# Split-operand products for Q, K, V and Wo, column-tiled gates and an earlier bias fold in a transformer and MoE kernel

## The chip, the cores and the metric

One core of a Trainium2 chip (trn2). The time is the device time of one execution in microseconds: 970.05 for the kernel before, the median of 3 runs (969.35 to 970.36).

## The reference

Video is 8 x 512 x 256 in f32. Two layers follow one another: linear attention with random features (16 heads of 16, 64 features a head) with a feed-forward part behind it, and a mixture of 8 experts. Around the parts stand layer norms and residuals. Cut to what matters:

```python
q = split(video @ Wq.T + bq); k = split(video @ Wk.T + bk); v = split(video @ Wv.T + bv)
qp = softmax_kernel(q, proj, is_query=True)      # 16 heads, 64 features each
kp = softmax_kernel(k, proj, is_query=False)
k_sum = jnp.sum(kp, axis=2)
denom = jnp.einsum('bhnm,bhm->bhn', qp, k_sum)
ctx = jnp.einsum('bhnm,bhnd->bhmd', kp, v)
out = jnp.einsum('bhnm,bhmd->bhnd', qp, ctx) / denom[..., None]
attn = out.transpose(0, 2, 1, 3).reshape(b, n, d) @ Wo.T + bo
x = layer_norm(video + attn, g2, be2)
ff = jax.nn.relu(x @ W1.T + b1) @ W2.T + b2
y = layer_norm(x + ff, g3, be3)
...
scores = jax.nn.softmax(xf @ gate_w.T, axis=-1)  # 8 experts
vals, idx = jax.lax.top_k(scores.T, k)           # 512 rows for each expert
# each expert: layer norm of its rows, fc1, gelu, fc2, times score, added at idx
```

## The kernel before

Tokens go in 8 batches of 512 (4 tiles of 128 tokens; 256 features are 2 tiles of 128). All five engines run programs of their own, ordered by semaphores. Each program is a loop over `body(i, f, u)`, a pipeline three batches deep: `i` is the batch in attention, `f` the batch in the feed-forward part (i - 1), `u` the batch in the last norm and the gates (i - 2). Bodies 0 and 1 and the last two lack some of the parts. The order inside a body is written out by hand on each engine, so an instruction that waits holds everything behind it on its engine. Behind the batches come the selection of 512 rows for each expert, the eight experts, and the last norm.

PSUM is cut into pA (2 banks, attention), pX (4 banks, random features, also written as pXall) and pF (2 banks, feed-forward and gates). pA and pF are handed on in turn: PE waits in `slot_a` and `slot_f` until the engine that takes the previous content has done so.

The order on PE around the change, in body i: K and Q (`by_features`, 512 columns, f32), V (`by_tokens`, 256 columns, f32), the turn of x2 of batch i - 1, the random features of k (`features`), two turns of heads, and between the further features the hidden layer of batch i - 1 in eight pieces (`hidden`, L1413, with `by_halves`), then its second product (`ff_out`), the maxima (`turn_kmax`, `spread_kmax`, `turn_tops`), the turned features, the context, the key sum (L1560), `attention_out` (L1434), the turns of xf and of oT, the gates (L1473), the turn of at, `turn_x(i + 1)`, and Wo (L1601). In body 0 the fold of be2 into the bias of the hidden layer stands at the end (L1602 to L1608: 32 instructions with one column each).

`by_halves` (L1378) takes operands that are split into an upper part, rounded to f32r, and a lower part, the rest. It sums three products: low x high, high x low, high x high. The hidden layer and the experts work like this; K, Q, V and Wo are plain f32 products.

VectorE (DVE) subtracts the lower halves (x2T_lo, L957), takes the maxima (L888, L917), subtracts the key bias (k_sub, L912), adds up statistics (L857, L861), writes xn (L882), x2, z and xf (L867), divides the heads (`heads_out`, L1010 and L1013), and adds r (L1049). `sums_of_context` (csum, csum_own, obias; L923 to L927) stands just ahead of xn in body 0. ScalarE (ACT) copies from PSUM (L474, L479, L484) and takes the exponentials. GpSimd (POOL) takes the roots (`root`, L719 and L721), sums kp over tokens (L770) and applies the scale and shift of the norms. In body 0, after `root(0, 1)`, it waits for the second fold_ready and then scales W1 by g2 and splits it:

```python
for c in range(C):
    nc.gpsimd.tensor_scalar(w1_raw[:, c], w1_raw[:, c], g2_c[:, c:c + 1], None, ALU.mult).then_inc(w1_split, 1)
pool.wait_ge(w1_split, C)
nc.gpsimd.tensor_copy(w1_hi[:], w1_raw).then_inc(w1_split, 1)
pool.wait_ge(w1_split, C + 1)
nc.gpsimd.tensor_tensor(w1_lo[:], w1_raw, w1_hi[:].bitcast(F32), ALU.subtract).then_inc(w1_split, 1)
```

Body 1 then adds be2 to b2 on POOL, takes `root(1, 0)` of the sum r of batch 0, and DVE makes x2 with it. `hidden(0)` of batch 0 waits for the split W1.

## Time and the profile before

| | |
|---|---|
| time, median of 3 | 970.05 us |
| profiled execution | 970.41 us, span 968.6 us |
| mean granted TensorE clock | 0.900 |
| PE busy | 762.2 us (79%), 5561 instructions |
| PE weight loads | 581.5 us (60%) |
| DVE busy | 595.6 us (61%) |
| ACT busy | 410.6 us (42%) |
| POOL busy | 352.9 us (36%) |
| chain that ended last | PE 62%, DVE 13%, DMA 6%, ACT 6%, POOL 6%, issue 5% |

Busy times are averages over stages. The attention and feed-forward stage reaches to about 630 us, the selection to about 700, the experts to about 925. The chain is followed back from the last instruction, at each step to what released it or to the instruction before it on its engine.

### The profile page before, as it was taken

Reading aid. Unit: us, or ns where it says so; the run is one execution under the profiler, and the core shown is the slowest. Engines: PE = TensorE matmul, PEld = TensorE weight load, DVE = VectorE, ACT = ScalarE, POOL = GpSimd, SP = SyncE. Lnnn points to the kernel's source line nnn. Section 1 sums busy time; section 2 is a strip of 40 time slices with the busy share of each in tenths; the row PEclk is TensorE's granted clock in tenths of the full one; section 3 lists DMA queues with packets and bytes.
Section 4 is the critical chain, followed back from the end, with each engine's and each line's share of the span. In section 5 each row is a group of like instructions: output and inputs, shape, how many; then the busy total and the mean of one; then the engine's idle time right before and its main releaser. Section 6 shows DMA issues by size and latency. Waiting matters only on the chain.

```text
span 968.6 us, 15201 instructions
## 1 busy us (share of the span) xinstructions
PE 762.2 (79%) x5561; PEld 581.5 (60%) x5561; DVE 595.6 (61%) x1426; ACT 410.6 (42%) x594; POOL 352.9 (36%) x299
## 2 busy tenths in 40 slices
PE   5578999999999999999999967211459989999900
PEld 2345856767767758668577656211348888888800
DVE  2722735857857957848758562588836656666445
ACT  2632634735636536637447321100045434455324
POOL 3136333514416405425335151100134444544346
PEclk9798999999999999999999979555569999999955
DMA  7000010011011020110100102220053555555274
GB/s 208 1 23 1 1 45 1 2 66 46 23 44 44 22 84 3 48 61 0 65 23 1 66 23 83 71 94 0 7 169 92 153 132 170 138 132 135 31 213 150
DMA packets 61530, 64.63 MB, mean 67 GB/s; under 512 B 9264, under 2 KB 58160, under 8 KB 61488
## 3 DMA queue, kind: packets, MB, share of 16 engines
q1 hardware_dynamic: 54384, 55.37, 17.4%
q0 software_dynamic: 6144, 8.52, 5.0%
q8 instruction: 27, 0.44, 0.2%
q10 hardware_dynamic: 960, 0.17, 0.1%
q14 instruction: 15, 0.12, 0.0%
HBM read 42.95 MB, written 21.10 MB: 66 GB/s over the span
## 4 chain that ended last, share of the span: by engine, by line
PE 62%; DVE 13%; DMA 6%; ACT 6%; POOL 6%; issue 5%; POOLq 0%; DVEq 0%; SPq 0%; ACTq 0%
PE pF L1382 10%; PE pX L1660 10%; PE pF L1424 9%; PE pA L1368 6%; PE pA L1375 5%; PE pX L1464 5%; DMA xg<-row_scratch,idx_g 4%; PE pX L1393 4%; PE pA L1353 3%; DVE qe L1108 3%; PE pX L1382 3%; POOL xg L799 2%; PE pA L1434 2%; PE pF L1477 2%; PE pF L1353 2%
## 5 line engine op out<-in xcount | busy, mean ns | idle before, releaser
L1424 PE MATMUL pF<-w,h 128*128 128x256 f32 x512 | 116.0, 380 | 0.0
L1424 PEld LDWEIGHTS pF<-w,h 128*128 128x128 f32 x512 | 95.6, 190 | 13.8 <-issue 1.4
L719 POOL TENSOR_SCALAR ve<-mv 128x4 f32<-128x4 f32 x40 | 9.1, 228 | 247.0 <-DVE mv L861 246.4
L807 POOL DMA_INDIRECT acc_scratch<-at,idx_s x32 | 51.6, 1613 | 107.3 <-DVE at L1216 100.6
L799 POOL DMA_INDIRECT xg<-row_scratch,idx_g x32 | 47.3, 1478 | 99.0 <-issue 86.0
L630 ACT ACTIVATE h<-pX,b1cur 128x512 f32<-128x512 f32 x64 | 44.1, 690 | 88.9 <-DVE b1cur L1227 75.4
L1660 PE MATMUL pX<-w_lo,h_hi 128*128 128x256 f32 x256 | 73.7, 288 | 0.8 <-issue 0.8
L1660 PE MATMUL pX<-w_hi,h_lo 128*128 128x256 f32 x256 | 73.0, 285 | 0.0
L1660 PE MATMUL pX<-w_hi,h_hi 128*128 128x256 f32 x256 | 72.9, 285 | 0.0
L867 DVE TENSOR_SCALAR z<-z,mv,rstd 128x256 f32<-128x256 f32 x64 | 62.3, 1034 | 7.0 <-POOL rstd L721 7.0
L479 ACT ACTIVATE h<-pF,b1c 128x512 f32<-128x512 f32 x64 | 44.2, 691 | 48.4 <-PE pF L1382 48.4
L1199 DVE TENSOR_TENSOR h_lo<-h,h_hi 128x512 fp32r<-128x512 f32 x64 | 42.9, 690 | 30.5 <-ACT h_hi L622 30.5
L1382 PE MATMUL pF<-x2T_hi,w_lo 128*128 128x512 f32 x128 | 55.1, 430 | 1.4 <-DVE x2T_lo L957 1.4
L1382 PE MATMUL pX<-x2T_hi,w_lo 128*128 128x512 f32 x128 | 51.8, 405 | 2.8 <-DVE x2T_lo L1248 2.8
L1382 PE MATMUL pX<-x2T_lo,w_hi 128*128 128x512 f32 x128 | 51.6, 403 | 0.0
L1382 PE MATMUL pF<-x2T_hi,w_hi 128*128 128x512 f32 x128 | 51.5, 403 | 0.0
L1382 PE MATMUL pX<-x2T_hi,w_hi 128*128 128x512 f32 x128 | 51.4, 401 | 0.0
L1382 PE MATMUL pF<-x2T_lo,w_hi 128*128 128x512 f32 x128 | 51.2, 400 | 0.0
L1660 PEld LDWEIGHTS pX<-w_lo,h_hi 128*128 128x128 f32 x256 | 49.7, 194 | 1.4 <-issue 1.4
L888 DVE TENSOR_REDUCE mxk<-kp 128x16 f32<-128x1024 f32 x32 | 37.3, 1209 | 21.4 <-ACT kp L489 21.4
L1660 PEld LDWEIGHTS pX<-w_hi,h_lo 128*128 128x128 f32 x256 | 49.7, 194 | 0.0
L1660 PEld LDWEIGHTS pX<-w_hi,h_hi 128*128 128x128 f32 x256 | 49.6, 194 | 0.0
(260 smaller groups left out, 1860.0 us busy)
## 6 DMA issues: line engine op xcount, KB each, us to landing
kp<-fc1T SPq DMA_DIRECT2D x8, 1024.0 KB, 7.9
w<-fc2T SPq DMA_DIRECT2D x8, 1024.0 KB, 8.0
xin<-video SPq DMA_DIRECT2D x8, 512.0 KB, 3.9
x<-video SPq DMA_DIRECT2D x8, 512.0 KB, 4.5
x_scratch<-x SPq DMA_DIRECT2D x8, 512.0 KB, 2.9
acc_scratch<-xf SPq DMA_DIRECT2D x8, 512.0 KB, 3.0
row_scratch<-y SPq DMA_DIRECT2D x8, 512.0 KB, 3.0
qp<-x_scratch SPq DMA_DIRECT2D x2, 1024.0 KB, 10.5
```

The lines of the kernel that those rows point to most:

```text
L479: nc.scalar.activation(dst, pF[n % 2][:], func, **kw).then_inc(done, 1)
L630: nc.scalar.activation(h[:, n, :], pM[n % M_SLOTS], ACT.Gelu_apprx_tanh, bias=b1cur[:, n:n + 1]).then_inc(he_ready, 1)
L799: pool.indirect_dma_start(xg[:, g, :], None, row_d, bass.IndirectOffsetOnAxis(ap=idx_g[:, g:g + 1], axis=0)).then_inc(gathered, 16)
L807: pool.indirect_dma_start(acc_d, bass.IndirectOffsetOnAxis(ap=idx_s[:, g:g + 1], axis=0), og[:, g, :], None, compute_op=ALU.add).then_inc( ...
L867: ins = nc.vector.tensor_scalar(dst[:, t, :], src[:, t, :], mv[k][:, t, 0:1], rstd[k][:, t:t + 1], ALU.subtract, ALU.mult)
L1353: return nc.tensor.transpose(dst, src, ident[:])
L1368: ins = nc.tensor.matmul(dst[:, t2 * D:(t2 + 1) * D], xt[:, k, tok(2 * m + t2)], w[:, k, :], start=(k == 0), stop=(k == ks - 1))
L1375: ins = nc.tensor.matmul(dst[:], w[:, k, tok(n)], xt[:, k, :], start=(k == 0), stop=(k == ks - 1))
L1382: ins = nc.tensor.matmul(dst[:], w_[:, k, tok(n)], x_[:, k, :], start=(m == 0), stop=(m == len(parts) - 1))
L1424: ins = nc.tensor.matmul(slots[m][:, half * D:(half + 1) * D], h[:, k, tok(2 * m + half)], w2[:, k, :], start=(k == 0), stop=(k == FC - 1))
L1464: ins = nc.tensor.matmul(pXall[:, a, :], w_[rows], x_[rows], start=(n == 0), stop=(n == 2), tile_position=(32 * a, 0))
L1660: ins = nc.tensor.matmul(pM[2 + m][:, t2 * D:(t2 + 1) * D], h_[:, k, tok(2 * m + t2)], w_[:, k, :], start=(k == 0 and j == 0), stop=(k == ...
```

## The change

Q, K, V and Wo are computed as three f32r products of split operands. The weights are split once at the start: ACT copies the upper halves after all four raw weights have come (now into qp's memory), DVE subtracts. x and the heads (aT) are split in each batch: ACT's copy gives the upper half, two DVE subtractions each the lower one. Wo's result and the turned x go to the four-bank buffer pX instead of pA. The gates take 32 columns of weights, four token tiles side by side in four column tiles, with the experts along the partitions; DVE copies the result and PE turns it back (`turn_gates`). The fold of be2 moves from the end of body 0 on PE to a place behind `spread_kmax` of the same body, and DVE's addition of it with it, behind bo_b. v and the turned xf get places in qe, aT_hi and aT_lo take the place of xT and v, xT_hi and xT_lo share memory with x2T_hi and x2T_lo, and in the expert stage xg lies in kp and xga in oT. The diff, without the renamed semaphores and tensors:

```diff
-        wq, wk, wv, wo = (sb(n, [P, C, D]) for n in ("wq", "wk", "wv", "wo"))
+        wq_hi, wk_hi, wv_hi, wo_hi = (sb(n, [P, C, D], F32R) for n in ("wq_hi", "wk_hi", "wv_hi", "wo_hi"))
+        wq_lo, wk_lo, wv_lo, wo_lo = (sb(n, [P, C, D], F32R) for n in ("wq_lo", "wk_lo", "wv_lo", "wo_lo"))
-        gate = sb("gate", [P, C, P])
+        gate = sb("gate", [P, C, 32])
...
+        wq, wk, wv, wo = (qp[:].rearrange("p a b -> p (a b)")[:, k * C * D:(k + 1) * C * D].rearrange("p (c n) -> p c n", c=C)
+                          for k in range(4))
+        xfT = qe[:].rearrange("p a b -> p (a b)")[:, 4 * N:6 * N].rearrange("p (c n) -> p c n", c=C)
+        v = qe[:].rearrange("p a b -> p (a b)")[:, 6 * N:8 * N].rearrange("p (t d) -> p t d", t=TT)
...
+        xT_hi, xT_lo = x2T_hi, x2T_lo
+        gT = sb("gT", [P, P])
...
-        xgT_hi, xgT_lo, xga = x2T_hi, x2T_lo, aT
+        xgT_hi, xgT_lo, xga = x2T_hi, x2T_lo, oT[:, 0:C]
-        xg = sb("xg", [P, GT, ROW])
+        xg = kp_f[:, 0:GT * ROW].rearrange("p (g r) -> p g r", g=GT)
...
-                sp.dma_start(w[:], src.rearrange("(c p) n -> p c n", p=P)).then_inc(done, 16)
+            for w, src in ((wk, WkT), (wq, WqT), (wv, WvT), (wo, WoT)):
+                sp.dma_start(w, src.rearrange("(c p) n -> p c n", p=P)).then_inc(wqkvo_in, 16)
...
-                    nc.scalar.activation(xT[:, c, :], pA[c][:], ACT.Copy).then_inc(xT_ready, 1)
+                    nc.scalar.activation(xT_hi[:, c, :], pXall[:, c, :], ACT.Copy).then_inc(xT_ready, 1)
...
+                    if isinstance(i, int) and i == 0:
+                        act.wait_ge(wlo_ready, 4)
                     exp_q(i, 0)
                     exp_q(i, 1)
...
+            act.wait_ge(wqkvo_in, 16 * 4)
+            for hi, w in ((wk_hi, wk), (wq_hi, wq), (wv_hi, wv), (wo_hi, wo)):
+                nc.scalar.activation(hi[:], w, ACT.Copy).then_inc(whi_ready, 1)
             act.wait_ge(const_ready, N_CONST)
             xT_copy(0)
             act.wait_ge(bqk_in, 16 * 2)
...
+            def rest_of_weight(n, w, lo, hi):
+
+                dve.wait_ge(whi_ready, n + 1)
+                nc.vector.tensor_tensor(lo[:], w, hi[:].bitcast(F32), ALU.subtract).then_inc(wlo_ready, 1)
+
+            def rest_of_x(i):
+                for c in range(C):
+                    dve.wait_ge(xT_ready, i * C + c + 1)
+                    nc.vector.tensor_tensor(xT_lo[:, c, :], pXall[:, c, :], xT_hi[:, c, :].bitcast(F32), ALU.subtract).then_inc(xl_ready, 1)
+
+            def rest_of_heads(i):
+
+                for c in range(C):
+                    dve.wait_ge(aT_ready, i * C + c + 1)
+                    nc.vector.tensor_tensor(aT_lo[:, c, :], pA[(J_AT + c) % 2][:], aT_hi[:, c, :].bitcast(F32), ALU.subtract).then_inc(al_ready, 1)
...
                     if isinstance(i, int) and i == 0:
                         dve.wait_ge(fold_ready, 1)
                         nc.vector.tensor_tensor(bo_b[:], bo_b[:], pF[1][:, 0:D], ALU.add).then_inc(bias_ready, 1)
+                        dve.wait_ge(wff_in, 16 * N_WFF)
+                        dve.wait_ge(fold_ready, 2)
+                        nc.vector.tensor_tensor(b1c[:], b1c[:], pF[0][:, 0:FC], ALU.add).then_inc(bias_ready, 1)
...
-                    for m in range(2):
-                        dve.wait_ge(u_ready, u * U_JOBS + J_G + m + 1)
-                        nc.vector.tensor_copy(lg[:, 2 * m:2 * m + 2, :],
-                                              pF[m][:, 0:2 * P].rearrange("p (a b) -> p a b", a=2)[:, :, 0:E]).then_inc(lg_ready, 1)
-                    dve.wait_ge(lg_ready, 2 * (u + 1))
-                    su.link(nc.vector.tensor_reduce(lmx[:], lg[:], AX_X, ALU.max))
-                    nc.vector.tensor_tensor(lg[:], lg[:], lmx[:].unsqueeze(2).to_broadcast([P, TT, E]), ALU.subtract).then_inc(ls_ready, 1)
+                    dve.wait_ge(u_ready, u * U_JOBS + J_G + 1)
+                    nc.vector.tensor_copy(gT[:], pF[0][:, 0:P]).then_inc(lg_ready, 1)
+                if i is not None:
+                    rest_of_heads(i)
+                if more:
+                    rest_of_x(i + 1)
+                if u is not None:
+                    dve.wait_ge(u_ready, u * U_JOBS + J_G + 2)
+                    logits = pF[1][:, 0:P].rearrange("p (t x) -> p t x", t=TT)[:, :, 0:E]
+                    su.link(nc.vector.tensor_reduce(lmx[:], logits, AX_X, ALU.max))
+                    nc.vector.tensor_tensor(lg[:], logits, lmx[:].unsqueeze(2).to_broadcast([P, TT, E]), ALU.subtract).then_inc(lg_ready, 1)
                 if i is not None:
                     dve.wait_ge(xnb_ready, i + 1)
                     for m in range(2):
                         dve.wait_ge(a_ready, i * A_JOBS + J_WO + m + 1)
-                        nc.vector.tensor_tensor(r[:, 2 * m:2 * m + 2, :], pA[m][:].rearrange("p (a b) -> p a b", a=2),
+                        nc.vector.tensor_tensor(r[:, 2 * m:2 * m + 2, :], pXall[:, 2 + m, :].rearrange("p (a b) -> p a b", a=2),
                                                 xnb[:, 2 * m:2 * m + 2, :], ALU.add).then_inc(r_ready, 1)
                     sa.end()
...
-                if isinstance(i, int) and i == 0:
-                    dve.wait_ge(wff_in, 16 * N_WFF)
-                    dve.wait_ge(fold_ready, 2)
-                    nc.vector.tensor_tensor(b1c[:], b1c[:], pF[0][:, 0:FC], ALU.add).then_inc(bias_ready, 1)
 
             ln1_stats(0)
             ln1_norm(0)
+            rest_of_weight(0, wk, wk_lo, wk_hi)
             dve.wait_ge(wproj_in, 16 * HG)
             nc.vector.tensor_scalar(projbd[:], projbd[:], NORM, None, ALU.mult).then_inc(proj_ready, 1)
+            rest_of_x(0)
+            rest_of_weight(1, wq, wq_lo, wq_hi)
+            rest_of_weight(2, wv, wv_lo, wv_hi)
+            rest_of_weight(3, wo, wo_lo, wo_hi)
             dve.wait_ge(bvo_in, 16 * 2)
...
-                       + [(aT_ready, 2, c) for c in range(2)] + [(r_ready, 2, m) for m in range(2)])
+                       + [(al_ready, 2, c) for c in range(2)] + [(r_ready, 2, m) for m in range(2)])
...
             def slot_a(i, n):
 
-                if J_WO <= n and not (isinstance(i, int) and i == B - 1):
-                    pe.wait_ge(xT_ready, (i + 1) * C + n - J_WO + 1)
-                elif n < 2:
-                    s, per, k = a_taker[A_JOBS + n - 2]
+                if J_WO <= n:
+
+                    return pXall[:, 2 + n - J_WO, :]
+                if n < 2:
+                    s, per, k = a_taker[J_AT + n]
                     wait(pe, s, (i - 1) * per + k + 1)
                 else:
                     s, per, k = a_taker[n - 2]
@@ -1319,10 +1354,9 @@
             def turn_x(i):
 
                 pe.wait_ge(xn_ready, (i + 1) * TT)
+                wait(pe, qp_ready, i * G)
                 for c in range(C):
-
-                    wait(pe, aT_ready, (i - 1) * C + c + 1)
-                    turn_tokens(pA[c], xn, c).then_inc(t_ready, 1)
+                    turn_tokens(pXall[:, c, :], xn, c).then_inc(t_ready, 1)
...
             def slot_x(i, n):
 
                 if n == J_XK:
-                    wait(pe, qp_ready, i * G)
+                    pe.wait_ge(xl_ready, (i + 1) * C)
+                    wait(pe, r_ready, i * 2)
...
-            def by_tokens(dst, xt, w, m, ks):
-
+            def by_tokens(dst, x_hi, x_lo, w_hi, w_lo, m):
+
+                parts = [(k, x_, w_) for x_, w_ in ((x_hi, w_lo), (x_hi, w_hi), (x_lo, w_hi)) for k in range(C)]
                 for t2 in range(2):
-                    for k in range(ks):
-                        ins = nc.tensor.matmul(dst[:, t2 * D:(t2 + 1) * D], xt[:, k, tok(2 * m + t2)], w[:, k, :],
-                                               start=(k == 0), stop=(k == ks - 1))
-                return ins
-
-            def by_features(dst, w, xt, n, ks):
-
-                for k in range(ks):
-                    ins = nc.tensor.matmul(dst[:], w[:, k, tok(n)], xt[:, k, :], start=(k == 0), stop=(k == ks - 1))
+                    for j, (k, x_, w_) in enumerate(parts):
+                        ins = nc.tensor.matmul(dst[:, t2 * D:(t2 + 1) * D], x_[:, k, tok(2 * m + t2)], w_[:, k, :],
+                                               start=(j == 0), stop=(j == len(parts) - 1))
                 return ins
...
-                def gates(m):
-                    s = slot_f(f, u, "u", J_G + m)
-                    for t2 in range(2):
-                        for c in range(C):
-                            ins = nc.tensor.matmul(s[:, tok(t2)], xfT[:, c, tok(2 * m + t2)], gate[:, c, :],
-                                                   start=(c == 0), stop=(c == C - 1))
+                def gates():
+
+                    s = slot_f(f, u, "u", J_G)
+                    for c in range(C):
+                        for t in range(TT):
+                            ins = nc.tensor.matmul(s[32 * t:32 * t + 32, 0:P], gate[:, c, :], xfT[:, c, tok(t)],
+                                                   start=(c == 0), stop=(c == C - 1), tile_position=(0, 32 * t))
                     ins.then_inc(u_ready, 1)
 
+                def turn_gates():
+
+                    s = slot_f(f, u, "u", J_G + 1)
+                    pe.wait_ge(lg_ready, 2 * u + 1)
+                    turn(s[:, 0:P], gT[:]).then_inc(u_ready, 1)
+
                 at_first(f, pe)
                 if att:
                     pe.wait_ge(xT_ready, (i + 1) * C)
-                    for j0, w, w_in in ((J_K, wk, wk_in), (J_Q, wq, wq_in)):
-                        first_batch(w_in)
+                    pe.wait_ge(xl_ready, (i + 1) * C)
+                    for n, (j0, hi, lo) in enumerate(((J_K, wk_hi, wk_lo), (J_Q, wq_hi, wq_lo))):
+                        first_batch(wlo_ready, n + 1)
                         for c in range(G):
-                            by_features(slot_a(i, j0 + c), w, xT, c, C).then_inc(a_ready, 1)
-                    first_batch(wv_in)
+                            by_halves(slot_a(i, j0 + c), hi, lo, xT_hi, xT_lo, c).then_inc(a_ready, 1)
+                    first_batch(wlo_ready, 3)
                     for m in range(2):
-                        by_tokens(slot_a(i, J_V + m), xT, wv, m, C).then_inc(a_ready, 1)
+                        by_tokens(slot_a(i, J_V + m), xT_hi, xT_lo, wv_hi, wv_lo, m).then_inc(a_ready, 1)
...
+                    if isinstance(i, int) and i == 0:
+                        pe.wait_ge(w1_in, 16)
+                        pe.wait_ge(wff_in, 16 * N_WFF)
+                        for n in range(FC):
+                            for c in range(C):
+                                ins = nc.tensor.matmul(pF[0][:, n:n + 1], w1_raw[:, c, tok(n)], be2_c[:, c:c + 1], start=(c == 0), stop=(c == C - 1))
+                        ins.then_inc(fold_ready, 1)
...
                 if gt_:
                     pe.wait_ge(xfT_ready, (u + 1) * C)
-                    gates(0)
-                    gates(1)
+                    gates()
                 if att:
                     pe.wait_ge(at_ready, (i + 1) * TT)
                     for c in range(C):
                         turn_tokens(slot_a(i, J_AT + c), at, c).then_inc(a_ready, 1)
                     if not (isinstance(i, int) and i == B - 1):
                         turn_x(i + 1)
+                if gt_:
+                    turn_gates()
+                if att:
                     pe.wait_ge(aT_ready, (i + 1) * C)
-                    first_batch(wo_in)
+                    first_batch(wlo_ready, 4)
                     for m in range(2):
-                        by_tokens(slot_a(i, J_WO + m), aT, wo, m, C).then_inc(a_ready, 1)
-                if isinstance(i, int) and i == 0:
-                    pe.wait_ge(w1_in, 16)
-                    pe.wait_ge(wff_in, 16 * N_WFF)
-                    for n in range(FC):
-                        for c in range(C):
-                            ins = nc.tensor.matmul(pF[0][:, n:n + 1], w1_raw[:, c, tok(n)], be2_c[:, c:c + 1], start=(c == 0), stop=(c == C - 1))
-                    ins.then_inc(fold_ready, 1)
+                        if m == 0:
+                            pe.wait_ge(al_ready, (i + 1) * C)
+                        by_tokens(slot_a(i, J_WO + m), aT_hi, aT_lo, wo_hi, wo_lo, m).then_inc(a_ready, 1)
```

## Rows read from the trace of the kernel before

**Rows 1.** Chain that ended last, middle batches: start us, us, what (x instructions)

```profile
216.65 3.69 PE pA L1368 x16
...
264.14 0.57 PE pA L1560 x16
...
280.26 1.79 PE pF L1477 x16
282.05 0.45 PE pA L1353 x4
...
284.58 3.72 PE pA L1368 x16
288.30 6.87 PE pA L1375 x16
295.17 3.45 PE pA L1368 x16
```

**Rows 2.** The same chain in the expert stage

```profile
729.84 11.71 PE pX L1660 x96
```

**Rows 3.** Timeline of DVE, middle batch: start us, us, then idle before it

```profile
293.86 1.35 DVE L867 TENSOR_SCALAR x<-r,mv,rstd 128x256 f32<-128x256 f32 x4
...
299.77 1.29 DVE L957 TENSOR_TENSOR x2T_lo<-pF,x2T_hi 128x512 fp32r<-128x512 f32 x2 [2.88 <-ACT x2T_hi L479]
...
322.47 7.68 DVE L867 TENSOR_SCALAR z<-z,mv,rstd 128x256 f32<-128x256 f32 x4
...
348.55 0.42 DVE L1013 TENSOR_TENSOR at<-pA,rden 128x256 f32<-128x256 f32 x1
```

**Rows 4.** Timeline of ACT, middle batch

```profile
350.48 1.08 ACT L474 ACTIVATE aT<-pA 128x512 f32<-128x512 f32 x2 [3.95 <-PE pA L1353]
```

**Rows 5.** Timeline of POOL, middle batch

```profile
322.02 2.76 POOL L770 TENSOR_TENSOR sq<-kp 128x1024 f32<-128x1024 f32 x1 [8.63 <-ACT kp L515]
324.86 4.82 POOL L770 TENSOR_TENSOR sq<-sq,kp 128x1024 f32<-128x1024 f32 x2
```

**Rows 6.** Chain that ended last, batches 0 and 1

```profile
11.40 1.28 ACT L484
...
13.83 8.66 PE pA L1375 x16
...
43.33 1.13 PE pX L1353 x4
...
74.11 3.48 PE pF L1607 x32
77.76 5.69 POOL h L781 x2
...
85.49 4.52 POOL w_lo L785
...
93.74 1.97 PE pF L1353 x8
...
99.32 2.80 PE pF L1382 x12
```

**Rows 7.** Timeline of DVE in batch 0

```profile
60.49 1.46 DVE L882 TENSOR_SCALAR xn<-xin,mv,rstd 128x256 f32<-128x256 f32 x4
64.82 0.26 DVE L1010 RECIPROCAL rden<-pA 128x16 f32<-128x16 f32 x1 [2.88 <-PE pA L1353]
```

**Rows 8.** Timeline of POOL in batch 0

```profile
55.92 1.05 POOL L721 TENSOR_TENSOR rstd<-ve,mhalf 128x4 f32<-128x4 f32 x1
```

**Rows 9.** Windows: stretch, length, then each engine's busy us, granted clock, DMA

```profile
38.00:45.00 7.00, 1.39 (x10) 0.88 (x5) 6.58 (x7) 4.82 (x6) 0.00 (x0) 0.50 0.00 0
```

**Rows 10.** Chain that ended last, behind the last batch

```profile
623.99 3.79 PE pF L1477 x16
```

**Rows 11.** Instructions and transfers of tile wo

```profile
L401 SPq DMA_DIRECT2D wo<-WoT x1: 473/473/473, 2.9 to 2.9; - x1
...
DMA to landing us min/median/max: 5.5/5.5/5.5
```

More of the change, by code:

```diff
@@ L252, in build, with early @@
         with ExitStack() as first_stages:
-            def early(name, shape):
-                return first_stages.enter_context(nc.sbuf_tensor(name, shape, F32))
+            def early(name, shape, dt=F32):
+                return first_stages.enter_context(nc.sbuf_tensor(name, shape, dt))
             xin = early("xin", [P, TT, D])
@@ L258, in build @@
             xnb = early("xnb", [P, TT, D])
-            xT = early("xT", [P, C, N])
+            aT_hi = early("aT_hi", [P, C, N], F32R)
+            aT_lo = early("aT_lo", [P, C, N], F32R)
             kT = early("kT", [P, G, N])
             qT = early("qT", [P, G, N])
-            v = early("v", [P, TT, D])
             r = early("r", [P, TT, D])
@@ L278, in build @@
         vel, rsl, nmr = (sq_f[:, 384 + 64 * n:384 + 64 * n + B * TT].rearrange("p (k t) -> p k t", k=B) for n in range(3))
-        wk_in, wq_in, wv_in, wo_in = (sem(f"w{n}_in") for n in "kqvo")
+        wqkvo_in, whi_ready, wlo_ready = sem("wqkvo_in"), sem("whi_ready"), sem("wlo_ready")
+        xl_ready, al_ready = sem("xl_ready"), sem("al_ready")
         bqk_in, bvo_in = sem("bqk_in"), sem("bvo_in")
@@ L310, in build @@
         xfT_ready, lg_ready = sem("xfT_ready"), sem("lg_ready")
-        ls_ready, le_ready, sc_ready = sem("ls_ready"), sem("le_ready"), sem("sc_ready")
+        le_ready, sc_ready = sem("le_ready"), sem("sc_ready")
         x1_out, xf_out, y_out, sc_out = sem("x1_out"), sem("xf_out"), sem("y_out"), sem("sc_out")
@@ L399, in _ @@
             load_x(0)
-            for w, src, done in ((wk, WkT, wk_in), (wq, WqT, wq_in), (wv, WvT, wv_in), (wo, WoT, wo_in)):
-                sp.dma_start(w[:], src.rearrange("(c p) n -> p c n", p=P)).then_inc(done, 16)
+            for w, src in ((wk, WkT), (wq, WqT), (wv, WvT), (wo, WoT)):
+                sp.dma_start(w, src.rearrange("(c p) n -> p c n", p=P)).then_inc(wqkvo_in, 16)
             sp.dma_start(w1_raw, W1T.rearrange("(c p) n -> p c n", p=P)).then_inc(w1_in, 16)
@@ L597, in body @@
                     for c in range(C):
-                        take_a(i, J_AT + c, aT[:, c, :], ACT.Copy, aT_ready)
+                        take_a(i, J_AT + c, aT_hi[:, c, :], ACT.Copy, aT_ready)
                     if not (isinstance(i, int) and i == B - 1):
@@ L1406, in body, with first_batch @@
                 att, ff, gt_ = i is not None, f is not None, u is not None
-                def first_batch(w_in):
+                def first_batch(ready, value):
                     if isinstance(i, int) and i == 0:
-                        pe.wait_ge(w_in, 16)
+                        pe.wait_ge(ready, value)
                 def hidden(n):
@@ L1511, in body @@
                     if isinstance(i, int) and i == 0:
-                        pe.wait_ge(wo_in, 16)
+                        pe.wait_ge(wqkvo_in, 16 * 4)
                         pe.wait_ge(proj_ready, 2)
```

4 lines of the change are left out of this document (1 added, 3 removed).

## The prediction

> **What bounds the kernel now.** I read the page first: TensorE (PE) is the busiest engine, and its share of the chain that ended last is the largest. A share over the whole span mixes stages, so the next view was that chain in order of time. In a middle batch [rows 1] the reader is to see that it runs from one PE line straight into the next: the product with Wo (3.72 us), K and Q (6.87), V (3.45), then the feed-forward part. There every microsecond taken from PE comes off the time, unless another engine is then late. The timelines of VectorE (DVE) and ScalarE (ACT) of the same batch say how late they could be [rows 3, 4]. The selection and expert stages behind 630 us are not touched. The one large hole of the attention stage lies between batch 0 and batch 1 [rows 6]: PE computes the bias fold (3.48 us), then GpSimd (POOL) scales and splits W1 from 77.76 to 90.0 us, and PE turns x2 at 93.74.
>
> **K, Q, V and Wo as split products.** Before, each product of 128x512 is one f32 matmul, issued as two instructions: 16 instructions in 6.87 us, 0.43 each, or 0.86 a product. The hidden layer already has the new form, f32r matmuls of 512 columns: 12 in 2.80 us, 0.233 each [rows 6]. K and Q need 24: 5.60 us, a gain of 1.27. With 256 columns the nearest row is the experts' second product, 96 in 11.71 us, 0.122 each [rows 2]. V's 24 take 2.93 us instead of 3.45, a gain of 0.52, and Wo's the same. A gain of 1.79 ahead of each batch and of 0.52 at its end.
>
> Who pays for the lower halves? ACT copies as before. DVE gets four subtractions of 128x512 a batch, a pair of which takes 1.29 us (the same form on x2T) [rows 3]. They stand between at and the sum r, where DVE waits for PE. With T the start of the turn of at (282.05 in this batch), Wo starts at T+2.53 today, held by the two aT copies and two xT copies through the same two banks. After: both aT copies are done about T+1.6 (they begin at 350.48, one period of 67.93 after T+0.5, and take 1.08 [rows 4]), the second lower half 0.65 to 1.0 later, so T+2.3 to T+2.6: no change. The second lower half of x is ready near T+4.0, and Wo ends at about T+5.7, so K does not wait. The edit costs nothing for as long as Wo covers it; bare, it would be 1.3 us a batch. v and the turned xf move into the free tail of qe and the raw weights into qp, with no wait of their own in the loop.
>
> What is late next? x2. DVE has it ready at 295.2, 6.9 us behind Wo's end (288.30); PE asks for it 8.5 us behind Wo's end, when K, Q and V take 5.60 and 2.93. So 1.6 us of slack are left of 3.4. Everything behind V hangs on PE (k_max, exp, POOL's key sums, the blocked DVE stretch at 322.47) and moves along with it. I count the 1.79 whole. The last batch has no next x to turn: there Wo waits some 0.85 us longer for the lower halves.
>
> **Gates as column tiles.** 1.79 us of PE between the last turn of oT and the turn of at [rows 1]. In the new form 16 instructions of 32 columns of weights go side by side; the nearest row is the key sum's 16 in 0.57 us. PE then waits for the last at of DVE, which starts at 348.55 and takes 0.42 [rows 3], so T comes at 349.05 to 349.2 and not at 350.0 (282.05 and a period): a gain of 0.8 and not 1.2. The extra copy (a quarter microsecond) and turn lie in the gap ahead of Wo. Bounds: 0, if the tiles ran one behind another, and 1.2. I take 0.8. Here one page speaks against the edit: the Trainium skill, TensorEngine Tiling (Array Packing), Restrictions, says that column tiling switches the fast weight load off. The key sum's 0.57 us is measured with column tiles and holds whatever that costs. If the rule took the whole gain, the sum below would be 4 us smaller.
>
> Behind the last batch the gates stand alone on the chain: 3.79 us at the low clock [rows 10]. New: 16 short instructions at half pace (1.15), a copy, one turn and their hand-overs (0.75), so 1.9 gained; one batch earlier, at full clock, 0.9.
>
> **The start.** ACT now waits for all four weights. The last is issued at 2.9 and takes 5.5 [rows 11]: 8.4. Behind that wait ACT holds xT, for which PE waits. The table load (1.28, at 11.40 before) comes forward, four copies take about 2.0, so xT is copied from 11.7 instead of 12.7, and the lower halves of x are there at about 13.7; K started at 13.83 [rows 6]. No change. K to V are shorter by 1.8 as in the other batches.
>
> **The fold inside batch 0.** Its 32 matmuls now stand behind spread_kmax, in a hole ahead of turn_tops (43.33 [rows 6]): from 38 on PE is busy for 1.39 of 7 us, at a granted clock of 0.50, the 1.2 GHz level [rows 9]. At full clock they take 3.48 us and fit. At 1.2 GHz they would take up to 7.0 and end at 43.6, where turn_tops stood ready at 41.5 (43.3 less 1.8): up to 1.9 us late, which eats the start's gain. I take 1.9. DVE waits for this fold too, with the statistics of batch 1 behind it in its queue and POOL's root(0, 1) behind those; but it is busy with k_sub until about then, so that wait costs it at most half a microsecond.
>
> Then POOL. It is free after root(0, 1), 55.92 + 1.05 [rows 8], less 1.8: 55.2. Its W1 work takes 12.2 us (77.76 to 90.0), so it ends at about 67.4 instead of 90.0. But it now lies on top of DVE's csum_own and of the four xn instructions behind it (60.49, 1.46 in all) [rows 7], and the heads of batch 0 stand behind them in DVE's queue. What such an overlap does is in the steady batch: four z instructions of that very form took 7.68 us while POOL added on 128x1024 from 322.02 to 329.7 [rows 3, 5]. One DVE instruction got through for each POOL instruction. So in batch 0: csum_own about 61, xn(0) behind the cast at 63, xn(1) behind the 4.52 us of w1_lo, xn(2) behind the small b2 sum, xn(3) at 68.6 (with 0.5 for POOL's own stretching). Heads begin at 68.6 instead of 64.82; four take 2.7, so T = 71.3. PE has idled and runs at 1.2 GHz: the 16 turns take 3.9 (8 took 1.97 at 93.74), Wo 3.5: 78.7. K, Q and V end at 87.2. x2 is ready at 84 to 85.6. PE turns x2 at 87.2 instead of 93.74, and at full clock it is at the hidden layer 2.9 later (an estimate, half of 5.58 and a little) instead of 5.58. Hidden(0) starts at 90.1 instead of 99.32: 9.2 gained, with every gain of batch 0 in it.
>
> For this block the trace has only POOL instructions with two inputs. If scaling and cast (one input) let DVE by, csum_own and xn pass at once: T = 67.7, full pace, hidden(0) at 84.7, 5.5 us earlier still. Bounds 9.2 and 14.7; I take the block, since its rows are the nearest. The Trainium skill, SBUF — State Buffer, Who interferes with whom, calls the port pair that the two engines share an exclusive lock, held for a whole instruction, and adds that a VectorE instruction with two SBUF inputs also contends with a GpSimd instruction that reads. By that rule all POOL steps here block, as I took it, and csum_own too. It gives no other time; against no block it is the 5.5 us.
>
> **The sum.** First batch up to hidden(0) 9.2; K, Q, V of batches 2 to 7 6 x 1.79 = 10.7; Wo and gates of batches 2 to 6 5 x 1.32 = 6.6, of the last 0.5 net; the two gates behind 2.8. Together 29.8 us. The profiled execution took 970.41 us (span 968.6 and 1.8 around it), 0.36 above the median: 940.6 on its scale, 940.2 beside the median. I say 940.
>
> **Rivals.** (1) No block in batch 0: 934.7. For it: one-input POOL work was not seen beside DVE. (2) The gain ahead of each batch is not passed on, since x2 or POOL's affine in front of stats(3) becomes late: 10.7 back, 951. For it: only 1.6 us of slack. Against: DVE idles before and behind it. (3) Slower than before: the wait between the turn of x and Wo, 0.8 us and new, or a queue that waits longer than I think, drops PE to 1.2 GHz at each hand-over. Wo, K, Q and V (11.7 us) would take twice as long in 7 batches: +82 - 30, 1022. It decides from 4.3 us of work at half pace per batch on (29.8 / 7). For it: the clock did fall in the hole at 38 to 45 [rows 9]. Against: gaps of 0.3 to 0.8 us in each batch left it at full pace, 3.45 us for V each time [rows 1].
>
> **Numbers.** A measurement tells 0.2% (2 us) from no change. Forecast 0.62; (1) 0.2; (2) 0.12; (3) 0.03; other small losses 0.03. 931 to 953 holds the forecast with its bounds (gates 0 or 1.2, fold 0 to 1.9, start within 1), (1) and (2), and leaves (3). All but (3) are faster: 0.96 faster, 0.01 within 0.2%, 0.03 slower.
>
> **What would show it.** K and Q near 5.6 us, V and Wo near 2.9 in the chain. Gates near 0.6, and T about 0.8 earlier. POOL's W1 work beginning near 55, xn of batch 1 stretched from about 1.5 to 7 us or more, heads of batch 0 near 68.6, hidden(0) near 90. Wo 2.6 us behind T. No PE wait for x2 in batches 2 to 7. I am wrong if PE waits for xT_lo, aT_lo or x2, if the middle batches shrink by less than 2.5 us (67.9 to about 64.8), or if POOL's W1 work starts much later.

## The result and the profile after

The changed kernel takes 938.73 us (median of 4 executions, 938.16 to 940.61) where the kernel before takes 970.20 (median of 4). The ratio is 0.9679, 95% interval 0.9662 to 0.9696: 31.5 us less, and 1.3 us below the forecast time of 940.

| | after |
|---|---|
| profiled execution | 938.94 us, span 937.2 us |
| mean granted TensorE clock | 0.893 |
| PE busy | 736.4 us (79%), 5761 instructions |
| PE weight loads | 584.6 us (62%) |
| DVE, ACT, POOL busy | 623.0 (66%), 412.6 (44%), 354.5 us (38%) |
| chain that ended last | PE 62%, DVE 16%, DMA 6%, ACT 5%, POOL 5%, issue 5% |

The page says that PE does 25.8 us less in 200 instructions more and that DVE does 27.4 us more. Where the time went is read in the chain that ended last. Its middle batch, for [rows 1] (start us, us, what):

```profile
204.85 3.11 PE pX L1404 x24
...
266.36 0.44 DVE at L1042
...
266.92 0.67 PE pA L1388 x4
...
267.61 0.61 ACT aT_hi L479
...
268.24 0.54 DVE aT_lo L938
...
268.85 0.69 DVE aT_lo L938
...
269.67 3.11 PE pX L1404 x24
272.78 5.61 PE pA L1412 x24
278.38 2.87 PE pA L1404 x24
281.25 0.87 PE pF L1388 x8
```

Wo took 3.72 us and takes 3.11, K and Q 6.87 and 5.61, V 3.45 and 2.87. PE goes from V into the turn of x2 with no gap, so x2 is not late. Two things are new. The gates are gone from the chain: the last heads run over DVE, and T (the start of the turn of at, 266.92) waits for DVE. Wo stands 2.75 us behind T, through both halves of aT_lo. The period is 269.67 less 204.85, 64.82 us; it was 67.93 (284.58 less 216.65 in [rows 1]). The parts add up: 0.83 at the gates (T is 0.96 behind their start, and was 1.79), 0.61, 1.26 and 0.58 at the products, less 0.22 between T and Wo, are 3.06 of the 3.11 (67.93 less 64.82).

The same batch in the timelines of PE and of DVE, with the idle time ahead in brackets:

```profile
265.96 0.64 PE L1508 MATMUL pF<-qe,gate 128*32 128x128 f32 x16
266.92 1.09 PE L1388 MATMUL pA<-ident,at 128*128 128x128 f32 x8 [0.31 <-DVE at L1042]
...
269.67 0.47 PE L1404 MATMUL pX<-wo_lo,aT_hi 128*128 128x256 f32 x2 [0.68 <-DVE aT_lo L938]
```

```profile
278.34 1.35 DVE L877 TENSOR_SCALAR x<-r,mv,rstd 128x256 f32<-128x256 f32 x4
```

The 16 instructions of the gates take 0.64 us, and PE then waits 0.31 for at and later 0.68 for aT_lo. x2 is complete at 279.69, and V ends near 281.2: 1.5 us of slack, where 1.6 was worked out.

The first batch, for [rows 6], in the same chain:

```profile
13.55 8.60 PE pA L1412 x24
...
37.18 6.92 PE pF L1575 x32
44.09 0.97 PE pX L1388 x4
...
60.84 8.15 DVE xn L892 x4
68.99 0.18 DVE rden L1039
...
71.65 1.97 PE pA L1388 x8
73.61 1.71 PE pX L1388 x8
75.32 4.05 PE pX L1404 x24
79.37 5.61 PE pA L1412 x24
84.98 2.88 PE pA L1404 x24
87.86 0.87 PE pF L1388 x8
...
90.86 2.80 PE pF L1412 x12
```

The windows, for [rows 9] (length, busy us of PE, PE's loads, DVE, ACT, POOL, granted clock, DMA):

```profile
38.00:45.00 7.00, 7.00 (x33) 6.65 (x33) 7.00 (x9) 4.30 (x4) 0.15 (x1) 0.50 0.00 0
...
70.00:74.00 4.00, 3.11 (x16) 2.66 (x15) 2.08 (x6) 0.95 (x2) 0.00 (x0) 0.61 0.39 131
```

The fold takes 6.92 us at the 1.2 GHz level (granted clock 0.50), where it took 3.48 [rows 6], and turn_tops waits for its end. Four xn instructions take 8.15 us where they took 1.46 [rows 7]. POOL and DVE side by side say why:

```profile
58.70 2.85 POOL L791 TENSOR_SCALAR h<-h,g_c 128x1024 f32<-128x1024 f32 x1
61.62 1.89 POOL L793 CAST w_hi<-h 128x2048 fp32r<-128x2048 f32 x1
63.59 4.52 POOL L795 TENSOR_TENSOR w_lo<-h,w_hi 128x2048 fp32r<-128x2048 f32 x1
```

```profile
60.42 0.17 DVE L951 TENSOR_TENSOR csum_own<-csum,epsmask 128x8 f32<-128x8 f32 x1
60.75 0.94 DVE L892 TENSOR_SCALAR xn<-xin,mv,rstd 128x256 f32<-128x256 f32 x1
61.62 2.04 DVE L892 TENSOR_SCALAR xn<-xin,mv,rstd 128x256 f32<-128x256 f32 x1
63.57 4.68 DVE L892 TENSOR_SCALAR xn<-xin,mv,rstd 128x256 f32<-128x256 f32 x1
68.18 0.81 DVE L892 TENSOR_SCALAR xn<-xin,mv,rstd 128x256 f32<-128x256 f32 x1
```

The first xn ends just behind POOL's second scaling (61.69 and 61.55), the second just behind the cast, the third just behind w1_lo: one DVE instruction for each of POOL's. This is the block that the prediction took. Csum_own ran beside the scaling in 0.17 us; the prediction had it blocked. The Trainium skill, SBUF — State Buffer, Who interferes with whom, has the shared port pair held for a whole instruction; the three ends agree with that, and csum_own (two SBUF inputs, beside a scaling that reads) does not; experiment 3 shows an xn that got through in the middle of such an instruction.

The turn of at and Wo of the last batch, in the chain of the kernel before and in that of the changed kernel:

```profile
553.74 0.45 PE pA L1353 x4
...
555.35 3.73 PE pA L1368 x16
```

```profile
526.00 0.67 PE pA L1388 x4
...
528.75 3.13 PE pX L1404 x24
```

Wo stands 2.75 us behind T, where it stood 1.61. Behind the last batch, for [rows 10], the chain of the last gates:

```profile
595.80 1.12 PE pF L1508 x16
...
597.87 0.20 DVE lmx L1076
```

From the gates to lmx (the maximum of the scores) 2.07 us, where it was 4.03; one batch earlier 1.49 instead of 2.30.

### The profile page after: what moved, and what is told of

Its sections match the earlier page's. It is cut to its first block, busy times and chain, and to the rows that moved or that the text cites. A ratio compares the mean times of both kernels' runs of the same rounds, so it can differ in the third digit from the quotient of the medians.

```text
span 937.2 us, 15655 instructions
## 1 busy us (share of the span) xinstructions
PE 736.4 (79%) x5761; PEld 584.6 (62%) x5761; DVE 623.0 (66%) x1454; ACT 412.6 (44%) x598; POOL 354.5 (38%) x299
## 4 chain that ended last, share of the span: by engine, by line
PE 62%; DVE 16%; DMA 6%; ACT 5%; issue 5%; POOL 5%; POOLq 0%; DVEq 0%; ACTq 0%; SPq 0%
PE pF L1412 10%; PE pX L1702 10%; PE pF L1454 10%; PE pX L1494 5%; PE pA L1412 5%; DMA kp<-row_scratch,idx_g 5%; PE pX L1423 4%; DVE qe L1142 3%; PE pX L1404 3%; POOL kp L809 3%; PE pX L1412 3%; PE pA L1388 3%; PE pA L1404 2%; PE pX L1388 2%; ACT qp L535 2%
## 5 line engine op out<-in xcount | busy, mean ns | idle before, releaser
L809 POOL DMA_INDIRECT kp<-row_scratch,idx_g x32 | 47.6, 1487 | 97.3 <-issue 84.1
L1233 DVE TENSOR_TENSOR h_lo<-h,h_hi 128x512 fp32r<-128x512 f32 x64 | 42.9, 690 | 29.8 <-ACT h_hi L632 27.0
L626 ACT ACTIVATE oT<-pX,lnb_c,lnw_c 128x512 f32<-128x512 f32 x16 | 12.3, 768 | 89.1 <-PE pX L1388 89.1
```

Of the source, the lines that this page charges most:

```text
L809: pool.indirect_dma_start(xg[:, g, :], None, row_d, bass.IndirectOffsetOnAxis(ap=idx_g[:, g:g + 1], axis=0)).then_inc(gathered, 16)
L1233: nc.vector.tensor_tensor(h_lo[:, n, :], h[:, n, :], h_hi[:, n, :].bitcast(F32), ALU.subtract).then_inc(h_lo_ready, 1)
```

## The experiments

Every kernel computes the whole result. Each was executed five times beside the kernel before (two of them six times), which stood at 969.8 to 971.3 us; times are medians, ratios are to the kernel before, and the diffs are cut, and against the changed kernel where nothing else is said. The changed kernel was not repeated beside them, so a difference to its 938.73 carries the 1.5 us by which the kernel before moved. Profiled executions scatter too where no experiment edits anything: from the start of the selection to the end they took 333.7 (e4_fold_split) to 338.5 us (e10_fold_split_late_lo), nearly all of it in the expert stage. Where hidden(0) or a period is given, it is free of that.

**1. Which part is worth what.** Four kernels put a part back, or keep one alone: the fold and its addition at the end of body 0 again (e1_fold_late), the gates in the old form (e5_old_gates), both (e6_products_alone), and the kernel before with nothing but the early fold (e9_fold_alone). The core of the first and of the second:

```diff
 def run_body(i): # PE
-    fold(0)   # 32 matmuls, behind spread_kmax
     turn_tops
     ...
     by_tokens(Wo)
+    fold(0)   # and b1c += pF[0] on DVE at the end of its body
```

```diff
-    s[32 * t:32 * t + 32, 0:P], gate[:, c, :], xfT[:, c, tok(t)], tile_position=(0, 32 * t)
+    s[:, tok(t2)], xfT[:, c, tok(2 * m + t2)], gate[:, c, :]   # m = 0, 1
```

> The changed kernel with the second fold (be2 into the hidden layer's bias) and its addition back at the end of body 0. Theory, the fold's place is worth what POOL's W1 work leaves bare: without the fold in the hole the turn of at of batch 0 starts near 66.7 us, Wo ends near 72.5, the fold near 76, POOL's W1 work near 88.3, x2 is turned near 92 at the low clock, and hidden(0) starts near 97.6 instead of 90.86: 6.7 us slower than the changed kernel, about 945.5. Rival, the first batch gained through the split products alone: within 2 us of the changed kernel's 938.7.

> The changed kernel with the gates as before (128 columns of weights, token tiles one behind another, no turn). Theory, the gates are worth 0.8 to 1.0 us in each of batches 2 to 7 and 2.8 behind them: the time is 7 to 8.5 us longer, 946 to 947. Rival, the turn of at was held by DVE's last at anyway: only the 2.8 behind the batches, 941.5.

> The changed kernel with both the gates and the second fold as before; of the change the split products, their buffers and the start are left. Theory, the parts add up: the products alone bring 970.2 down by 3.1 for each batch behind the first less the gates' 0.8 to 1.0, about 2.2 x 7, and nothing at the start: 954 to 955. Rival, the products' gain needs the other two (x2 late without the early fold, or the turn of at): 960 or more.

> The kernel before with the early second fold alone: f32 products and the old gates. Theory, the fold's place brings the same as in the changed kernel (7.9 us there, 946.6 against 938.7) less a little, since K, Q, V take 10.3 us instead of 8.5 and xn meets POOL's work at another point: xn is stretched to 8 us or more, hidden(0) starts near 94.5 instead of 99.32, and the time is 965 to 966. Rival, with f32 products the low clock or the block eats the gain: 969 or more.

| kernel | median us | ratio (95%) |
|---|---|---|
| e6_products_alone | 954.40 | 0.9849 (0.9826 to 0.9873) |
| e1_fold_late | 946.63 | 0.9760 (0.9741 to 0.9779) |
| e5_old_gates | 944.88 | 0.9731 (0.9709 to 0.9754) |
| changed kernel | 938.73 | 0.9679 (0.9662 to 0.9696) |
| e9_fold_alone | 967.28 | 0.9958 (0.9942 to 0.9974) |

The products alone give 15.8 us (970.2 less 954.40), the gates 7.8 behind them (954.40 less 946.63) or 6.2 as the last edit (944.88 less 938.73), the fold 7.9. The periods bear the first two out. From one T to the next in the middle they are 67.95 us before, 65.50 in e6_products_alone and in e5_old_gates, and 64.82 in the changed kernel, so 2.45 for the products and 0.68 for the gates. Two of the expectations missed: e5_old_gates lost 6.2 us and not 7 to 8.5, and e9_fold_alone stood at 967.28 and not at 965 to 966. The fold's value depends on the rest: alone it gives 4 (971.3 less 967.28). The chain of e1_fold_late behind its heads shows the order of before, with Wo at full pace and POOL behind the fold (the view ends inside the last line):

```profile
69.43 3.12 PE pX L1405 x24
72.55 4.50 PE pF L1650 x32
...
77.21 5.70 POOL h L791 x2
...
84.95 4.57 POOL w_lo L795
...
93.26 1.97 PE pF L1389 x8
...
98.97 2.11 PE pF L1413 x9
```

Hidden(0) at 98.97 against 90.86: the 8.1 us of the fold's place lie in the hole between batches 0 and 1. One of them is this execution's: the fold took 4.50 us here and 3.48 in e6_products_alone, where hidden(0) came at 97.25. The chain also says why the fold alone gives less. With the fold late, POOL's W1 work behind it sets hidden(0), and K, Q and V of batch 1 lie beside it: what the new products save in these is lost, 98.97 and 97.25 against 99.32 in [rows 6]. With the fold early they are on the path. The old products then bring hidden(0) to 96.83 in e9_fold_alone, the new ones to 90.86. Of these 6.0 us 1.6 are K and Q of batch 0, which took 10.17 us in e9_fold_alone, where the same 16 instructions had taken 8.66 in the kernel before; no run says why.

**2. Is it POOL's work that holds xn?** One kernel lets POOL's W1 work wait for the four xn (e2_pool_behind_xn), one cuts w1_lo in four (e3_w1_lo_in_four).

```diff
+                    pool.wait_ge(xn_ready, 2 * TT)
                     # scaling of W1, cast, w1_lo
```

```diff
-  nc.gpsimd.tensor_tensor(w1_lo[:], w1_raw, w1_hi[:].bitcast(F32), ALU.subtract).then_inc(w1_split, 1)
+  for c in range(C):
+      for q in range(2):
+          cols = slice(q * W, (q + 1) * W)   # W = FF // 2
+          ins = nc.gpsimd.tensor_tensor(w1_lo[:, c, cols], w1_raw[:, c, cols], w1_hi[:, c, cols].bitcast(F32), ALU.subtract)
+  ins.then_inc(w1_split, 1)
```

> The changed kernel, but POOL begins its W1 work only when xn of batch 1 is written. Theory, the block on DVE's xn holds the heads of batch 0: xn then takes 1.5 us instead of 8.2, the heads start near 66.5 (now held by the turns of oT, at the low clock) instead of 68.91, Wo runs at full pace, W1 is ready near 74.5 and hidden(0) does not wait for it: hidden(0) near 86.7 instead of 90.86, 4.2 us less, about 934.5. Rival, PE's low clock in the tail of batch 0 comes from the fold and not from the wait, so that the turns and Wo stay slow: only 2.3 us less, 936.4. Second rival, the later start of W1 work holds hidden(0): no gain or a loss.

> The changed kernel with POOL's w1_lo (4.52 us) issued as four instructions of a quarter each; nothing else is moved. Theory, one DVE instruction gets through for each POOL instruction: xn(2) waits for the first quarter and xn(3) for the second, so xn ends near 66 instead of 68.99, and hidden(0) comes 2.3 to 4 us earlier, 935 to 936.5. Rival, DVE is let through only when POOL's whole stretch of work ends: xn ends near 69 and the time stays at 938.7.

e2_pool_behind_xn took 933.69 us, ratio 0.9640 (0.9615 to 0.9665). DVE's timeline:

```profile
60.27 1.38 DVE L893 TENSOR_SCALAR xn<-xin,mv,rstd 128x256 f32<-128x256 f32 x4
64.61 0.26 DVE L1040 RECIPROCAL rden<-pA 128x16 f32<-128x16 f32 x1 [2.96 <-PE pA L1389]
```

Xn is back at 1.38 us, the heads wait for PE, as they did before [rows 7], and Wo takes 3.10 us with a granted clock of 1.00 from 68 to 74. POOL's work, from 61.85 on, is done at 74.19, long before PE asks for W1 at 84.7. So the whole of the block was avoidable: 5.0 us by the medians (one of the six executions took 940.15 and widens the interval), and 6.1 at hidden(0), 84.73 instead of 90.86, of which 0.85 lies ahead of the fold. e3_w1_lo_in_four took 936.12, 0.9650 (0.9631 to 0.967): xn took 5.19 us, and the last two of them 1.43 and 1.36, each to the end of a piece of w1_lo. Both expectations held.

**3. What opens the block?** The fold was split, 8 of its instructions ahead in the free stretch behind turn_kmax, 24 in the old place (e4_fold_split); the cast was written as a scaling by 1.0 (e8_cast_as_scalar); and the split was repeated with 4 and 28 (e12_fold_4_28).

```diff
+    if i == 0:   # PE, behind turn_kmax
+        for n in range(2):   # e12: range(1)
+            for c in range(C): matmul(pF[0][:, n:n + 1], ...)
     ...
-        for n in range(FC):
+        for n in range(2, FC):   # e12: range(1, FC)
```

```diff
-                    nc.gpsimd.tensor_copy(w1_hi[:], w1_raw).then_inc(w1_split, 1)
+                    nc.gpsimd.tensor_scalar(w1_hi[:], w1_raw, 1.0, None, ALU.mult).then_inc(w1_split, 1)
```

> The changed kernel with the second fold in two portions, 8 of its 32 instructions in the hole behind turn_kmax and 24 behind spread_kmax, so that turn_tops starts near 42.3 us instead of 44.09. Theory, POOL's work sets the start of the heads: hidden(0) and the time stay within 1 us of 938.7. Rival, PE's chain through the fold sets it: up to 1.8 us less, 936.9.

> The changed kernel, with POOL's cast of W1 to w1_hi written as a tensor_scalar with 1.0, the form of the scaling in front of it. The run with the split fold showed all four xn instructions passing beside the scaling, 0.4 to 1.2 us each. Theory, the scaling's form lets DVE through while the cast and the sum of two inputs do not: though this POOL instruction takes some 5.7 us instead of 1.9, xn passes beside it and ends near 64 instead of 69, the heads start near 65.9, and the time is 3 to 5 us shorter, 934 to 936. Rival, every POOL instruction lets one DVE instruction through and blocks the rest: xn(1) waits to 67 and xn(2) to 72, and the time is 3 to 4 us longer, 942.

> The changed kernel with the fold split 4 and 28 instructions, so that xn arrives about 0.9 to 1.3 us earlier than in the changed kernel, in the middle of POOL's second scaling instruction (in the run with 8 and 24 it came 2.4 us earlier and passed three times within that instruction, from 59.0 to 59.6). Theory A, that instruction lets DVE through in its middle: one or two xn pass at once, none waits for w1_lo, and the time is that of the 8 and 24 split, 932 to 934. Theory B, each POOL instruction lets one DVE instruction through whatever the point: xn ends near 68 and the time stays at 937 to 939.

e4_fold_split took 931.85 us, 0.9622 (0.9598 to 0.9645): 6.9 less than the changed kernel, where none was expected. Its five executions run from 929.72 to 936.83, and the profiled one, with hidden(0) at 83.78 instead of 90.86, is the fastest. Its POOL and its DVE:

```profile
57.76 2.84 POOL L791 TENSOR_SCALAR h<-h,g_c 128x1024 f32<-128x1024 f32 x1
```

```profile
57.84 1.19 DVE L892 TENSOR_SCALAR xn<-xin,mv,rstd 128x256 f32<-128x256 f32 x1
58.94 0.72 DVE L892 TENSOR_SCALAR xn<-xin,mv,rstd 128x256 f32<-128x256 f32 x2
59.59 1.16 DVE L892 TENSOR_SCALAR xn<-xin,mv,rstd 128x256 f32<-128x256 f32 x1
```

All four xn went through inside one POOL instruction: the first was held until 59.03, 1.27 us into it, two ran at their own 0.4 us, and the last was held to its end. So "one for each POOL instruction" is not the rule of a scaling, and neither is a hold for the whole instruction. The first reading of this, that a scaling lets DVE by and cast and w1_lo do not, fell with e8_cast_as_scalar: 942.50 us, 0.9720 (0.9706 to 0.9735), 3.8 more, as its rival had it. Its POOL and its DVE:

```profile
61.36 5.37 POOL L793 TENSOR_SCALAR w_hi<-h 128x2048 fp32r<-128x2048 f32 x1
```

```profile
61.34 5.53 DVE L892 TENSOR_SCALAR xn<-xin,mv,rstd 128x256 f32<-128x256 f32 x1
```

The cast as a scaling took 5.37 us instead of 1.89, and the xn beside it was held to its end.

What fits every profiled execution is an opening inside the scaling of 128x1024, told from the start of the second one (2.85 us long):

| kernel | DVE instruction | begins | what came of it |
|---|---|---|---|
| e4_fold_split | xn(0) | +0.08 | held until +1.27 |
| e10 (below) | csum_own | +0.40 | held until +1.13 |
| e10 | xn(0), xn(1) | +1.30, +1.62 | pass |
| e12_fold_4_28 | csum_own, xn(0) | +1.14, +1.48 | pass, 0.17 and 0.41 us |
| e4_fold_split | xn(1), xn(2) | +1.18, +1.51 | pass |
| changed kernel | csum_own | +1.72 | passes, 0.17 us |
| e4, e12, e10 | next xn | +1.83, +1.80, +1.95 | held to the end |
| changed kernel | xn(0) | +2.05 | held to the end |
| e8_cast_as_scalar | csum_own, then xn(0) | +2.11, +2.45 | passes, held |
| e9, e7, e3 | csum_own, then xn(0) | +1.87 to +2.06, +2.21 to +2.40 | passes, held |
| e5_old_gates | csum_own | +2.59 | passes, 0.17 us |

Xn of 0.4 us pass if they begin between 1.2 and 1.6 us into the scaling; the tiny csum_own (8 elements a partition) was held at 0.4 and still passed at 2.6. This also says why a shorter fold helps so much. POOL comes to W1 from its own key products and not from the fold; DVE's csum hangs on PE and so on the fold. In e4_fold_split W1's scaling begins 0.94 us earlier than in the changed kernel (54.92 and 55.86) and csum_own 2.93 us earlier (57.49 and 60.42), so that DVE meets the scaling 2.0 us earlier in its course; 1.7 of these are the fold's own (5.21 us for its second part instead of 6.92). e12_fold_4_28 stands between: 932.29 us (0.9595, 0.9579 to 0.9612), but its executions run from 930.13 to 937.12, and the profiled one, the slowest, has one xn through the opening and three held, the last of them until 67.91. That its other executions found more of the opening is argued from their times alone; they have no profile. Nor did any run tell what makes the opening; the table was read after the runs and foretold none of them. One more thing is in the 6.9 us. In e4_fold_split DVE's q work ahead of the fold ended at 33.87, and at 35.69 in the changed kernel, since K began at 12.87 and not 13.55 and K and Q of batch 0 took 7.47 us and not 8.60. At the fold's second part 0.96 us of this was left (36.22 and 37.18). No experiment but e9_fold_alone edits these products, and in their 24-instruction form they took 7.19 to 8.60 us over the profiled executions. By this scatter medians of different kernels can differ by a microsecond or more (an estimate).

**4. Can Wo start before aT_lo is there?** Each 256-column sum of Wo begins with four matmuls that need only aT_hi. The wait for aT_lo is moved behind them, for each half, in the first token tile.

```diff
+    if lo_ready is not None and t2 == 0 and x_ is x_lo:
+        pe.wait_ge(al_ready, lo_ready + k + 1)
...
-    if m == 0:
-        pe.wait_ge(al_ready, (i + 1) * C)
```

> The changed kernel, but Wo's first four matmuls of the first token tile, which read only aT_hi, go ahead of the wait for aT_lo. Theory, the lower halves of the heads hold Wo in every batch (0.68 us of PE waiting behind the turns): each of 7 batches gets 0.48 shorter, 3.4 us in all, 935.3. Rival, K of the next batch then waits for the lower half of x, or x2 becomes late: less than 1 us.

e7_late_wait_for_lo took 932.04 us, 0.9607 (0.9584 to 0.9631). Its chain:

```profile
263.75 1.09 PE pA L1388 x8
264.83 0.87 PE pX L1388 x8
...
265.82 3.13 PE pX L1406 x24
```

Wo stands right behind the turns, 2.07 us behind T instead of 2.75. So 0.68 us a batch, the whole wait that the timeline of PE showed, and not the 0.48 expected; over seven batches 4.8 of the 6.7 us by the medians. The rest stands ahead of hidden(0), 89.00 instead of 90.86: 0.85 us of it lies ahead of the fold, with K and Q of batch 0, and the rest goes with Wo of batch 0 (2.88 us instead of 4.05), where no run separates the edit from the clock.

**5. The versions together.** e10_fold_split_late_lo has the edits of e4 and e7; e11_split_late_lo_pool_last has POOL's wait of e2 as well.

> The changed kernel with the split fold and with Wo's first four matmuls ahead of the wait for aT_lo. Theory, they lie at different places and add: hidden(0) near 83, 0.7 us less in each batch behind it, 926 to 927. Rival, x2 becomes late when the sum of both is gone (1.4 us of slack before V's end were measured in the changed kernel): 930 or more.

> The same, and POOL starts its W1 work only when xn of batch 1 is written. Theory, with the split fold xn was no longer on the path (2.9 us instead of 8.2, the heads wait for the turns of oT), so this wait changes nothing: within 1 us of the run without it, 926 to 927. Rival, W1 ready later holds hidden(0): 1 us or more above it.

e10_fold_split_late_lo took 927.38 us, 0.9550 (0.9532 to 0.9568), 11.3 less than the changed kernel, and e11_split_late_lo_pool_last 927.31, 0.9543 (0.9526 to 0.9559). They are one time within what can be measured. The 6.9 and the 6.7 us of the two edits do not simply add up: 1.9 of the second lay ahead of hidden(0), and there e4_fold_split stands at 83.78 and e10 at 83.36. In e10 two xn pass in the opening, the fourth ends with the cast at 63.47, and DVE then still waits 0.46 us for PE, so keeping POOL back has nothing left to give.

## Why the prediction held, point by point

- **Products.** Held. Worked out: 1.79 us ahead of a batch and 0.52 at its end, 2.31. Measured: 1.26, 0.58 and 0.61, 2.45. e6_products_alone puts the part at 15.8 us; the sum's terms for it are 13.0 (six times 1.79, five times 0.52, less 0.3 net in the last batch), and its hidden(0) came 2.1 us earlier as well (97.25 for 99.32). K of batch 0 began at 13.55 for about 13.7. Batch 0 is the exception: K to V there were to be 1.8 us shorter and were 0.6 (25.04 less 13.55, against 25.94 less 13.83), since K and Q took 8.60 us for 8.66.
- **x2's slack.** Held: 1.5 us left against 1.6. Rival (2), which needed it to fail, would have ended at 951.
- **Between T and Wo.** Slightly wrong: 2.75 us, beyond the T+2.3 to T+2.6 and 0.22 more than before. The second aT_lo waits in DVE's queue behind the first, and PE needs 0.14 more. That costs some 1.5 us over seven batches; the whole 0.68 us wait of a batch could be removed (experiment 4).
- **Gates.** Held: 0.83 in a middle batch for 0.8, 0.81 for 0.9 and 1.96 for 1.9 behind. Of the 0.83 the period keeps 0.68 (65.50 with the gates put back, 64.82 without). Terms of 7.6 us stand against 6.2 and 7.8 by the medians. The 16 instructions took 0.64 us, near the key sum's 0.57, so no cost of the column tiles' weight loads is seen that the nearest row did not hold already.
- **Fold at the low clock.** Held: 6.92 us for 7.0, turn_tops at 44.09 for 43.6.
- **Block of xn.** Held as to cause and size for this execution: heads at 68.99 for 68.6, T at 71.65 for 71.3, and e2_pool_behind_xn shows rival (1)'s world with hidden(0) at 84.73, for 84.7 (its fold began 0.85 us earlier, which is K and Q of batch 0 again). Two of its steps were wrong: csum_own was not blocked, and xn began in POOL's second scaling, not behind it, so that one xn and not two was left behind w1_lo. The end moved little, since w1_lo held an xn either way. That the block would hold wherever xn falls was wrong too, as e4_fold_split shows. With the whole fold ahead of it xn(0) came 2.05 us or more after the start of the scaling in each profiled execution in which POOL's work lay over it, too late for an opening that the prediction did not know of; that it fell so was luck.
- **First batch.** 8.46 us against 9.2. K and Q, 1.2 us longer than worked out, brought POOL to W1 at 55.86 and not 55.2, and T came 0.35 late; Wo of batch 0 took 4.05 us and not 3.5, behind a stretch with the granted clock at 0.61 (70 to 74).
- **The sum.** It leaves out one term: Wo of batch 1 stands behind hidden(0) and belongs to no batch that it counts, 0.5 us. To T of the last batch 27.7 us were gained (553.74 less 526.00) against 27.3 (9.2 and six times 1.79, five times 1.32 and 0.8), or 27.9 with that term. Wo then waits 1.14 us longer there and not 0.85. To the turn of the gates' scores it is 30.1 against 29.8, at the end of the span 31.4. The last 1.3 us came in the selection and expert stages, where the change only moves two buffers; that is less than the 4.8 us by which the profiled executions differ there (333.7 to 338.5), so part of the nearness of 938.7 to 940 is luck. In rival (3) the sum of Wo, K, Q and V is 11.5 us by its own rows and not 11.7; nothing else rests on it.

## What to carry over

A product of an f32 operand as three f32r products pays when PE sets the time and the extra subtractions stand in another engine's idle time; look at what the first matmuls need, and put the wait for the lower halves behind those that don't need them. When work is moved into a hole, count it at the hole's clock and ask which other engine it sets free to collide: here the moved fold cost PE 7 us instead of 3.5, brought GpSimd's work onto VectorE's, and was worth 8 us all the same and 13 once the overlap was gone (946.63 less 933.69).

## What the runs showed of the hardware

- The same 32 matmuls with one moving column took 3.48 us behind Wo in the kernel before, 4.50 there in e1_fold_late, where the granted clock fell from 1.00 to 0.50 under them at about 75 us with PE busy since 69.43, and 6.92 in the hole. In the hole they kept PE busy for the whole of 38 to 45 us, and the granted clock reads 0.50 over that stretch, as it did when PE was busy for 1.39 us of it [rows 9].
- VectorE's tensor_scalar (128x256, 0.41 us) beside GpSimd's tensor_scalar of 128x1024 is held for part of it alone: free from about 1.2 to 1.6 us into its 2.85, held before and after. Beside GpSimd's cast (1.89), its tensor_scalar of 128x2048 (5.37) and its tensor_tensor (4.52) it was held to the end each time.
- A GpSimd cast of 128x2048 from f32 to f32r took 1.89 us, and 5.37 as a multiplication by 1.0.
- K and Q of batch 0, 24 instructions, took 7.19 to 8.60 us (the 16 f32 ones 8.66 and 10.17) in executions whose granted clock reads 1.00 for that stretch; in the changed kernel the instructions stand 0.43 us apart until 19.66 and 0.23 behind it, as in a middle batch.

Other VectorE instructions were not held beside GpSimd's. The statistics of 128x256 in the kernel before began 0.03 us into the first scaling of 128x1024 (77.76 to 80.62) and took 0.41 to 0.43 us each:

```profile
77.79 1.41 DVE L857 BATCH_NORM_STATS2 st<-r 128x6 f32<-128x256 f32 x4
```

The first aT_lo of batch 0, with one input from PSUM, took its usual 0.69 us beside the cast in e2_pool_behind_xn.
